# A DLRM tower on one core: first one-hot table in two halves, ids on another queue, some transposes and row products in another order

## The reference

```python
e = jnp.stack([tbl_0[ids[:, 0]], ..., tbl_25[ids[:, 25]]], axis=1)
combined = jnp.concatenate([e, r_dense_x[:, None, :]], axis=1)       # 512 x 27 x 128
interact = jnp.einsum('bfd,bgd->bfg', combined, combined)
z = interact[:, _TRIU_I, _TRIU_J]                                    # 351 pairs
h = jnp.concatenate([z, r_dense_x], axis=1)                          # 479
h = jnp.maximum(h @ W_top1 + b_top1, 0.0)                            # 512
h = jnp.maximum(h @ W_top2 + b_top2, 0.0)                            # 256
y = h @ W_top3
```

## Time and profile before

| what | us |
|---|---|
| median of three runs | 124.02 (123.65 to 124.3) |
| the profiled execution | 124.31 |
| its span, first to last instruction | 122.5 |
| PE busy | 112.3 (92%) |
| VectorE busy | 93.3 (76%) |
| GpSimd busy | 72.7 (59%) |
| ScalarE busy | 50.6 (41%) |

### The profile page before, as it was taken

One profiled execution on the slowest core, in us unless ns is written; L12 is line 12 of the kernel. 1 busy time (PEld: TensorE's weight loads), 2 busy tenths in 40 slices (PEclk: granted clock), 3 DMA queues, 4 the chain that ended last, 5 costly groups with the idle time before them and its releaser, 6 DMA issues. The chain is left out here.

```text
span 122.5 us, 2736 instructions
## 1 busy us (share of the span) xinstructions
PE 112.3 (92%) x794; PEld 88.1 (72%) x794; DVE 93.3 (76%) x377; ACT 50.6 (41%) x147; POOL 72.7 (59%) x80
## 2 busy tenths in 40 slices
PE   4758999999997999999999999999999969999990
PEld 4622445454643479977999899989997968998980
DVE  1079999999997995897799999980388995389312
ACT  4981323040605051892113793304488104387110
POOL 3488777777878878778778787787777700000000
PEclk9995999999999999999999999999999999999999
DMA  2899373645545418992222121121211200000000
GB/s 63 264 393 379 97 219 74 211 73 206 154 129 108 176 47 235 378 314 53 58 47 71 44 64 43 47 68 47 57 51 50 64 23 0 5 0 0 0 0 1
DMA packets 6398, 13.20 MB, mean 108 GB/s; under 512 B 2016, under 2 KB 3552, under 8 KB 6256
## 3 DMA queue, kind: packets, MB, share of 16 engines
q0 software_dynamic: 2336, 4.79, 15.6%
q1 hardware_dynamic: 3040, 5.44, 12.2%
q10 hardware_dynamic: 1008, 2.81, 7.8%
HBM read 13.03 MB, written 0.00 MB: 106 GB/s over the span
## 5 line engine op out<-in xcount | busy, mean ns | idle before, releaser
L306 POOL DMA_INDIRECT rows<-in_tbl_dram,idx x73 | 71.6, 981 | 24.2 <-issue 22.0
L408 DVE COPY PAIRS<-gram_ps 27x60 f32<-27x60 f32 (+1 forms) x96 | 24.3, 253 | 12.3 <-PE gram_ps L594 11.0
L351 ACT COPY XT<-turn_ps 128x512 f32<-128x512 f32 (+3 forms) x20 | 12.7, 647 | 42.2 <-PE turn_ps L557 25.4
L594 PE MATMUL gram_ps<-XT 128*123 128x80 f32 x256 | 28.5, 269 | 0.7 <-ACT XT L351 0.4
L594 PEld LDWEIGHTS gram_ps<-XT 128*123 128x123 f32 x256 | 27.9, 187 | 1.6 <-ACT XT L351 0.9
L351 ACT COPY PAIRS<-gram_ps 27x60 f32<-27x60 f32 (+1 forms) x96 | 23.4, 243 | 10.8 <-PE gram_ps L594 9.7
L484 DVE TENSOR_SCALAR onehot<-hot_ids,first_row 125x512 bf16<-125x512 int16 (+1 forms) x64 | 19.6, 378 | 5.8 <-DMA hot_ids<-in_hot_ids_dram 5.0
L433 DVE CUSTOM_DVE_ANT_0 few_prod<-rows 128x128 f32<-128x128 f32 x84 | 20.7, 290 | 0.8
L614 PE MATMUL h_ps<-PAIRS,W1P 128*128 128x128 f32 x130 | 16.9, 277 | 0.5 <-DVE PAIRS L408 0.5
L614 PEld LDWEIGHTS h_ps<-PAIRS,W1P 128*128 128x128 f32 x130 | 15.6, 192 | 0.9 <-ACT PAIRS L351 0.8
L557 PE MATMUL turn_ps<-onehot,hot_tab 125*128 125x512 bf16 (+3 forms) x64 | 13.4, 349 | 2.7 <-DVE onehot L484 2.0
(11 more groups left out here) (49 smaller groups left out, 75.6 us busy)
## 6 DMA issues: line engine op xcount, KB each, us to landing
hot_tab<-in_hot_dram ACTq DMA_DIRECT2D x5, 512.0 KB, 3.6
rows<-in_tbl_dram SPq DMA_DIRECT2D x128, 0.5 KB
hot_tab<-in_hot_dram SPq DMA_DIRECT2D x3, 512.0 KB, 8.0
W1P<-in_w_pairs_dram SPq DMA_DIRECT2D x1, 1280.0 KB
rows<-in_tbl_dram,idx POOLq DMA_INDIRECT x73
hot_ids<-in_hot_ids_dram SPq DMA_DIRECT2D x1, 640.0 KB, 8.1
W<-in_W_top_dram SPq DMA_DIRECT2D x1, 512.0 KB, 8.5
hot_ids<-in_hot_ids_dram SPq DMA_DIRECT2D x1, 256.0 KB, 5.7
```

The costliest lines, as they stand in the source:

```text
L306: pool.indirect_dma_start(rows[:, t, s, :], None, tables[f], bass.IndirectOffsetOnAxis(ap=idx[:, t, f:f + 1], axis=0)) \
L351: return nc.scalar.copy(dst, src)
L408: return nc.vector.tensor_copy(dst, src)
L594: last = nc.tensor.matmul(gram_ps[0:GRAM_ROWS, 2 * (i % 2) + q // fours, o:o + QUAD * NCOL], four.rearrange("d s f -> d (s f)")[:, 0:GRAM_ ...
```

## The change

Five edits; what is computed stays the same.

1. The load of `idx` goes from ScalarE's queue to the head of SP's. The ids of hot table 0 are then the first load on ScalarE's queue.
2. Hot table 0 is loaded in two halves of its columns (four of the eight pieces each), with a semaphore for the first. VectorE prepares each half in turn (four one-hot pieces, `hot_rest`, `hot_low`), and TensorE does the three passes of one half and then of the other.
3. The turn of group 6 of tile 0 moves from behind hot table 4 to behind hot table 5.
4. `turn_few` stands behind the third interaction batch in every tile.
5. Between the parts of tile 2's first layer, the turns of groups 5 and 3 of tile 3 change places; VectorE's copies follow the same order.

```diff
+HALF_COLS = CHUNKS * D // 2
-TURNS_AFTER = [[[1], [2, 3], [4, 5], [6]], [[1, 2], [3, 4], [5], []], [[1, 2], [3], [5], [4]]]
+TURNS_AFTER = [[[1], [2, 3], [4, 5], [6]], [[1, 2], [3, 4], [5], []], [[1, 2], [5], [3], [4]]]
-EARLY_TURNS = [[], [0], [1], [2, 3], [4, 5, 6], []]
+EARLY_TURNS = [[], [0], [1], [2, 3], [4, 5], [6]]
+        def half_of(half):
+            if half is None:
+                return range(CHUNKS), slice(0, 2 * HALF_COLS)
+            return range(half * CHUNKS // 2, (half + 1) * CHUNKS // 2), slice(half * HALF_COLS, (half + 1) * HALF_COLS)
+        def words_done(n, half):
+            return 1 if half == 0 else n + 2
+        def wait_table(eng, n, half):
+            if half == 0:
+                eng.wait_ge(hot_half_in, 16)
+            else:
+                eng.wait_ge(hot_in[n % RING], 16 * (n // RING + 1))
-            load_hot(sp, 0)
+            sp.dma_start(idx[:], ids).then_inc(idx_in, 16)
+            for half in range(2):
+                cols = slice(half * HALF_COLS, (half + 1) * HALF_COLS)
+                sp.dma_start(hot_tab[0][:, cols], hot_tables[0].rearrange("(p c) d -> p (c d)", c=CHUNKS)[:, cols]) \
+                    .then_inc(hot_half_in if half == 0 else hot_in[0], 16)
-            act.dma_start(idx[:], ids).then_inc(idx_in, 16)
+                for half in ([0, 1] if n == 0 else [None]):
+                    prepare_part(n, samples, half)
-                for part in range(FEW_PARTS):
+                for part, g in enumerate([g for g in ORDER[t + 1] if g % 2]):
                     few_pairs(t + 1, part)
-                    empty_bank(dve, copy, fill_no[("turn", t + 1, 2 * part + 1)])
+                    empty_bank(dve, copy, fill_no[("turn", t + 1, g)])
-                    for which in range(3):
+                    passes = [(half, which) for half in ([0, 1] if n == 0 else [None]) for which in range(3)]
+                    for half, which in passes:
             for t in range(TILES):
-                if t:
-                    turn_few(t)
                 for i in range(BATCHES):
                     gram(t, i)
-                    if t == 0 and i == FEW_AFTER:
+                    if i == FEW_AFTER:
                         turn_few(t)
```

More of the change, by code:

```diff
@@ L150, in build @@
         w3_in = sem("w3_in")
+        hot_half_in = sem("hot_half_in")
         hot_in = [sem(f"hot_in{i}") for i in range(RING)]
@@ L476, in prepare_table @@
                 part = slice(0, HOT_PARTS)
-                tab = hot_tab[n % RING][part, :]
                 if n >= 2:
@@ L481, in prepare_table, with prepare_part @@
                 dve.wait_ge([ids_first_in, ids_next_in, ids_next_in, ids_rest_in][min(n, 3)], 16)
-                for k in range(CHUNKS):
+                for half in ([0, 1] if n == 0 else [None]):
+                    prepare_part(n, samples, half)
+            def prepare_part(n, samples, half):
+                b = n % 2
+                part = slice(0, HOT_PARTS)
+                chunks, cols = half_of(half)
+                for k in chunks:
                     nc.vector.tensor_scalar(onehot[b][part, k, samples], hot_ids[part, n, samples],
@@ L486, in prepare_table @@
                                             ALU.add, ALU.is_equal).then_inc(onehot_ready, 1)
-                dve.wait_ge(hot_in[n % RING], 16 * (n // RING + 1))
+                wait_table(dve, n, half)
+                tab, rest = hot_tab[n % RING][part, cols], hot_rest[b][part, cols]
                 high = tab.bitcast(BF16)[:, 1::2]
[L490 to L495, removed]
+                nc.vector.tensor_tensor(rest, tab, high, ALU.subtract).then_inc(rest_ready, 1)
+                dve.wait_ge(rest_ready, words_done(n, half))
+                mid = rest.bitcast(BF16)[:, 1::2]
+                nc.vector.tensor_tensor(hot_low[b][part, cols], rest, mid, ALU.subtract).then_inc(low_ready, 1)
             dve.wait_ge(first_row_ready, 1)
@@ L543, in fill @@
                     words = [hot_tab[n % RING][part, :].bitcast(BF16), hot_rest[b][part, :].bitcast(BF16)]
-                    pe.wait_ge(hot_in[n % RING], 16 * (n // RING + 1))
-                    for which in range(3):
+                    passes = [(half, which) for half in ([0, 1] if n == 0 else [None]) for which in range(3)]
+                    for half, which in passes:
+                        if which == 0:
+                            wait_table(pe, n, half)
                         if which == 1:
-                            pe.wait_ge(rest_ready, n + 1)
+                            pe.wait_ge(rest_ready, words_done(n, half))
                         if which == 2:
-                            pe.wait_ge(low_ready, n + 1)
-                        for k in range(CHUNKS):
+                            pe.wait_ge(low_ready, words_done(n, half))
+                        for k in half_of(half)[0]:
                             if which == 0:
```

## The result

The changed kernel takes 120.64 us in the median of four runs (120.34 to 122.96), against 123.84 for the kernel before on the same chip: a ratio of 0.9732 [0.9683, 0.978]; ratios are made from the executions within 1.5% of the fastest of their kernel, so 122.96 here, and 168.93 and 172.09 in two of the experiments, do not enter them. The forecast was 120.8. The profiled execution took 120.48 us with a span of 118.7, against 124.31 and 122.5.

What follows compares the result with a forecast made beforehand. TensorE, busy 112.3 of 122.5 us, was taken as the bound, with waits and half clock to recover. 3.33 us at the last interaction less 0.1 gave 3.2: 124.31 to 121.1, less 0.29 to the median, 120.8; range 119.9 to 122.8.

Steps and rivals of the forecast that it cites:

- The start: First hot table: earlier ids and halves let TensorE run it from 5.4 to 10.6, 4.3 us won, net 4.0.
- The spread turns: Hot table 5 takes a long-emptied PSUM bank: 0.7 us gained, 0.1 given back, net 0.6.
- the first layer's weights: Tile 0's first layer: weights land at 54.3, TensorE waits from 52.3, so 2.6 of 4.6 us remain.
- The weights are early: Rival at tile 0's first layer: weights in at 53.4, 3.5 us remain, last gather decides, 120.5 us; chance 0.08.
- If a gather still holds tile 3's turns: Stated sign of a wrong forecast; group 3 was to cost no wait, group 4's gather to be in at 98.8.
- 99.95 in the sum: Forecast start of the last interaction, set by VectorE's last copy ending at 99.9, against 103.28 before: 3.33 us won.
- signs of being wrong: Three: no wait for the weights, the clock falling behind that wait, or a gather still holding tile 3's turns.
- the 0.15 us of edit 4: Row products behind the interaction: 0.1 lost in tile 1, 0.25 won in tile 2, making the shift 2.75 us.
- the wait for group 3 that edit 5 was to remove: In tile 3, TensorE's 1.03 us wait for group 3's gather, to vanish when groups 5 and 3 change places.
- 17.3 us to the end: Fixed work claimed behind the last interaction, from its start at 103.28 to the execution's end.
- The 0.1 us given back there: Behind tile 3's last interaction: row products moved into a 0.18 us wait, 0.1 us lost (0 to 0.25).
- P: Experiments' theory, not the prediction's: TensorE's own program sets the end; row waits are incidental; one gather less wins 0 to 0.3.

Runs made afterwards that it cites:

- the second execution: The changed kernel run once more without any edit, as the measure for runs beside it: 120.83 us, 0.9793 of the kernel before.
- one gather less: Changed kernel with tile 0's group 6 gather replaced by one plain load on SP's queue: 119.49 us, 0.9682 of the kernel before.
- earlier ids: Changed kernel with hot table 0's ids moved from ScalarE's queue to behind `idx` on SP's: 119.64 us, 0.9678 of the kernel before.
- work moved ahead of group 4: Changed kernel with tile 2's group 4 turned one first-layer part later, beside group 5: 120.99 us, 0.9793 of the kernel before.
- 1.5 us lost at the start: Changed kernel with `idx` back at the head of ScalarE's queue, ahead of hot table 0's ids: 121.28 us, 0.9809 of the kernel before.
- pause: Changed kernel with a GpSimd memset of 1024 or 2048 columns between `idx` landing and first gather: 121.21 us (0.9824) and 121.73 us (0.9863).
- The whole table's profiled execution: Changed kernel with hot table 0 loaded and prepared whole instead of in halves: 121.01 us, 0.9789 of the kernel before.
- run 340: Not a run label: "run" is the verb here, and 340 counts the gathers beside VectorE's `hot_rest` or `hot_low`; no measured time belongs to it.

## Why the prediction was right, and the step that failed

**The start** came as worked out: hot ids at VectorE at 3.92 (3.9), TensorE's first pass at 5.17 without a wait (5.4), the second table at 11.23 (10.9 by the sum of 4.0). The difference is in the first four matmuls, 1.91 us against 1.06 for the next four, although none of them waits. The profile (columns as in the earlier trace rows) gives the stretch a granted clock of 1.00:

```profile
5.20:6.90 1.70, 1.70 (x6) 0.60 (x5) 1.67 (x4) 1.70 (x2) 1.11 (x2) 1.00 0.88 259
```

Yet they follow each other by (6.88 - 5.17) / 4 = 0.43 us, the later ones by 0.22. With edit 1 undone the same matmuls go at 0.42 us from 8.18 to 9.86, where the granted clock is 0.50. So these four have the pace of the lower level, whatever the profile gives; why, stays open. In the second execution the same four took 1.16, so it is not a fixed price. So 3.66 was won instead of 4.0. The half-speed stretch of the earlier trace rows is gone. That reading of the start needs the same care: in edit 5 alone and in edits 3, 4 and 5 alone, which have the old head, the granted clock is 1.00 from 9.00 to 12.30, but the first pass goes at 0.41 and 0.42 us a matmul, and hot table 1 starts at 14.06 and 15.35.

**The spread turns**: the wait for the bank is gone, as forecast. TensorE starts interaction 0 at 41.29, against 45.83: 4.54 won, where 4.6 was forecast.

**The step that failed: the first layer's weights.** It put them in at 54.3 and let TensorE wait 2.0 us, so that 2.6 of 4.6 us remain. SP's part was taken as 0.3: `W1P` was started 46.09 - 45.29 = 0.80 later, the upper bound given (0.21 later in the second execution). But the transfer was taken from the bias behind the weights, as the only row there, and at the duration of before. `W1D` landed at 46.53 + 6.2 = 52.7, the bias at 46.98 + 6.0 = 53.0 instead of 46.26 + 7.8 = 54.06. TensorE waited 0.29, and 4.1 us were won there, not 2.6. That both loads are faster goes with the new head: `W1D` takes 6.0 to 6.8 us in six other traces that have it and show it, 7.1 with one gather less, which adds a load to it, and 8.0 and 8.1 in the two that have the old one. From edit 5 alone:

```profile
W1D<-in_w_dense_dram SPq DMA_DIRECT2D x1, 256.0 KB, 8.1
```

Why stays open; no run was made for it. "The weights are early" was a rival with a chance of 0.08.

**What took its place: the gathers.** "If a gather still holds tile 3's turns" was named as what would make the prediction wrong, and it does. They were taken 0.7 us earlier because `idx` is first in its queue, and group 4's as in by 98.8 (the last landed at 98.41). The first gather came 0.14 earlier (0.56 in the second execution), the last 97.03 - 95.71 = 1.32, mostly because the chain was shorter: (97.03 - 4.40) / 72 = 1.286 us per gather before, (95.71 - 4.26) / 72 = 1.270 after. The last one's lag, taken as at most 1.5 us, is 98.55 - (95.71 + 1.01) = 1.83. That bound took the end of data movement for the landing: in the changed kernel the DMA engines move nothing from 98.00 to 98.40 (share 0.00), and the landing comes at 98.41. What the forecast missed is how much slack the gathers had: by the lag of 2.70 from start to landing, the last one of the kernel before was in at about 99.7 (an estimate) and turned at 102.43. The slack of 2.7 and the 1.3 by which the last gather came earlier are 4.0 us, and TensorE came for it 102.43 - (98.55 - 0.64) = 4.52 sooner. The interaction thus started at 99.42, against 99.95 in the sum and 99.65 in the rival with early weights.

So two errors met: a wait of 2.0 us forecast at the weights that was not there, and waits of 0.74 and 0.64 for gathers that were not forecast. The sum is 0.5 us off at the interaction (3.86 won, 3.33 forecast). That the median was hit to 0.2 us is in part luck. Of its own signs of being wrong, two came: the wait for the weights is not there, and a gather still holds tile 3's turns. For edits 4 and 5 the order came as described, but the 0.15 us of edit 4 and the wait for group 3 that edit 5 was to remove are not shown to be worth anything at the end.

Behind the last interaction the prediction spoke of 17.3 us to the end; the rows give 122.5 - 103.28 = 19.2 of span before and 118.7 - 99.42 = 19.3 after. The figure was no term of the sum. The 0.1 us given back there was 0.06.

Shown by experiments: in the changed kernel the gathers set the end. One gather less and earlier ids won 1.3 and 1.2 us where P allowed 0.3, with nothing gained at TensorE's start; work moved ahead of group 4 won nothing; 1.5 us lost at the start cost 0.2. The rest of the kernel stands some 1.2 to 1.3 us behind. That the chain's length differs between the two executions is made up by its long gathers (below); why those are long is only argued.

## What to carry to other kernels

When a gain at the start passes through several engines, list every chain that runs beside the one made faster, with its slack at the end: here TensorE won 4.1 us by its first layer, GpSimd's chain had been moved by 0.14 to 0.6 us at its start, and the end followed GpSimd. A wait of before is no price for its removal unless it is also the last to end: taking away 1.03 us of waiting was worth nothing in the median here. Do not take a transfer's duration over from before when the change moves what is under way beside it.

## What the runs showed of the hardware

**A small load and its company.** With `idx` (52 KB) at the head of ScalarE's queue or of SP's, and another load at the head of the other, `idx` landed after 2.8 to 3.5 us and the first gather (with no pause ahead) started at 3.80 to 4.58; with the other queue empty it landed after 1.8 and the gather started at 2.80, in one trace. The Trainium skill ("DMA: Bandwidth & Descriptors", Queues, rings and completion order) says that an engine takes from its queues in turn, packet by packet; the traces are in line with that. Which of the two queues `idx` heads makes no difference that shows: 3.80 and 4.40 to 4.58 on ScalarE's, 3.82 to 4.31 on SP's.

**A wait can cost the clock.** With tile 2's turns spread, TensorE and the stretch behind its wait:

```profile
76.70 0.75 PE L598 MATMUL turn_ps<-ident,rows 128*128 128x128 f32 x3 [1.50 <-DMA rows<-in_tbl_dram,idx]
```

```profile
77.70:81.00 3.30, 3.30 (x17) 2.36 (x16) 0.17 (x1) 0.00 (x0) 2.38 (x4) 0.50 0.19 45
```

The whole table's profiled execution shows the same, 0.50 from 76.60 to 79.80 after 1.66 us. But in the changed kernel again the 1.60 us at the same place were followed by ten matmuls in 1.28 us and a granted clock of 1.00 from 76.00 to 83.00, against 2.34 us for ten at 0.50. The clock also stayed after 1.20 us ahead of group 3 of tile 3 in edits 1 and 2 alone, and after 0.74 and 0.64 in the changed kernel. So the length of the wait alone does not tell, at 1.5 to 1.7 us; what else decides is not shown.

**Long gathers.** Most gathers take 0.94 to 1.05 us, but a few take 1.2 to 1.8: 31 in the fourteen traces, 25 of them beside VectorE's `hot_rest` or `hot_low`. Beside these two run 340 gathers in all, so most are not stretched. GpSimd in the changed kernel run again:

```profile
61.47 1.62 POOL L329 DMA_INDIRECT rows<-in_tbl_dram,idx  x1 [0.30 <-issue]
63.39 0.95 POOL L329 DMA_INDIRECT rows<-in_tbl_dram,idx  x1 [0.30 <-issue]
```

VectorE:

```profile
61.06 1.21 DVE L520 TENSOR_TENSOR hot_rest<-hot_tab 125x1024 f32<-125x1024 f32 x1
62.30 1.23 DVE L524 TENSOR_TENSOR hot_low<-hot_rest 125x1024 bf16<-125x1024 f32 x1
```

The Trainium skill ("SBUF — State Buffer", SBUF: two separate sides) tells of a port pair that VectorE and GpSimd share: a VectorE operation with two SBUF inputs, as these have, locks it for the whole instruction against a GpSimd operation that reads SBUF. That a gather is such an operation no run here shows; the rows above would fit it, the many gathers that are not stretched show that it is not the rule. It is a coincidence in time, and no run separated the two. Above 0.94 us each, the long gathers lose 0.35 us in the changed kernel's trace and 1.41 in the second execution's, which makes up the 0.99 between the two chains. An estimate of what could be won by giving these two operations to another engine is therefore no more than that, and less where the rest of the kernel becomes the bound.
